# Softmax reciprocals spread through a row in HBM, and a sixth pair of heads in split fp32r products, in a fused attention and MLP layer

## The reference

```python
h = _layernorm(x) * (1 + ca) + sa
x = x + ga * attn(h)          # 16 query heads of 64, 4 key/value heads, rotary embedding
h = _layernorm(x) * (1 + cb) + sb
x = x + gb * ffn(h)           # binarised 128 -> 512 -> 128, exact gelu
# in attn: softmax(q k^T / 8) v, heads joined, @ Wo + bo
```

## Time and profile before

| | |
|---|---|
| median of three runs | 700.91 us (699.69 to 700.97) |
| profiled execution, its own time | 700.25 us |
| its span, first to last instruction | 698.5 us |
| PE matmul busy | 668.9 us, 96% |
| ACT busy | 551.4 us, 79% |
| DVE busy | 516.5 us, 74% |
| POOL busy | 430.1 us, 62% |
| DMA traffic on the SP queue | 24.40 MB |

### The profile page before, as it was taken

One profiled execution on the slowest core, in us unless ns is written; L12 is line 12 of the kernel. 1 busy time (PEld: TensorE's weight loads), 2 busy tenths in 40 slices (PEclk: granted clock), 3 DMA queues, 4 the chain that ended last, 5 costly groups with the idle time before them and its releaser, 6 DMA issues.

```text
span 698.5 us, 13530 instructions
## 1 busy us (share of the span) xinstructions
PE 668.9 (96%) x3733; PEld 519.5 (74%) x3733; DVE 516.5 (74%) x1196; ACT 551.4 (79%) x1149; POOL 430.1 (62%) x397
## 2 busy tenths in 40 slices
PE   4698999999999999999999999999999999998897
PEld 3566787877777787878787777778787878667786
DVE  6566777778788777777787778887777877778762
ACT  4478887888787888878887878787887888768676
POOL 1657685857686776768585768577676758543110
PEclk9699999999999999999999999999999999999999
DMA  8111111011111111111102111111111110200111
GB/s 241 31 32 33 33 26 39 18 38 28 32 31 32 32 20 29 32 32 32 31 16 43 20 32 31 32 32 28 26 27 33 32 34 18 48 17 3 39 39 46
DMA packets 31580, 24.75 MB, mean 35 GB/s; under 512 B 16688, under 2 KB 26944, under 8 KB 31552
## 3 DMA queue, kind: packets, MB, share of 16 engines
q1 hardware_dynamic: 31552, 24.40, 16.6%
HBM read 4.47 MB, written 2.10 MB: 9 GB/s over the span
## 4 chain that ended last, share of the span: by engine, by line
PE 90%; DVE 3%; ACT 3%; POOL 1%; issue 1%; DMA 0%; SPq 0%; POOLq 0%; DVEq 0%
PE o_ps L1021 15%; PE o_ps L1011 11%; PE unit_ps L957 9%; PE score_ps L992 8%; PE unit_ps L946 8%; PE score_ps L994 8%; PE unit_ps L973 8%; PE o_ps L1078 4%; PE unit_ps L931 3%; PE unit_ps L932 3%; PE unit_ps L933 3%; PE unit_ps L967 2%; PE unit_ps L961 2%; PE unit_ps L1055 1%; PE unit_ps L1056 1%
## 5 line engine op out<-in xcount | busy, mean ns | idle before, releaser
L521 POOL TENSOR_TENSOR probs_lo<-probs,probs_hi 128x512 fp32r<-128x512 f32 x160 | 202.1, 1283 | 67.7 <-ACT probs_hi L662 67.6
L772 DVE TENSOR_REDUCE w_all<-unit_ps 128x2 f32<-128x512 f32 x256 | 166.2, 685 | 52.4 <-PE unit_ps L957 50.9
L659 ACT ACTIVATE probs<-score_ps 128x512 f32<-128x512 f32 x256 | 150.6, 589 | 21.2 <-PE score_ps L994 18.6
L507 POOL TENSOR_TENSOR rot_sum<-rot_a,rot_b 128x512 f32<-128x512 f32 (+1 forms) x96 | 104.7, 1097 | 99.3 <-DVE rot_b L764 99.0
L511 POOL TENSOR_TENSOR qk_rot<-rot_sum,qk_rot 128x512 fp32r<-128x512 f32 (+1 forms) x96 | 105.0, 1101 | 36.3 <-ACT qk_rot L609 36.3
L957 PEld LDWEIGHTS unit_ps<-k_hi,q_hilo 128*128 128x128 f32 x512 | 88.7, 191 | 41.3 <-issue 17.9
L957 PE MATMUL unit_ps<-k_hi,q_hilo 128*128 128x256 f32 x512 | 118.3, 318 | 0.7 <-ACT q_hilo L591 0.4
L946 PEld LDWEIGHTS unit_ps<-ident_r,qk_rot 128*128 128x128 f32 x640 | 101.9, 194 | 17.7 <-issue 4.3
L946 PE MATMUL unit_ps<-ident_r,qk_rot 128*128 128x128 f32 x640 | 110.2, 264 | 4.6 <-POOL qk_rot L511 3.8
L992 PE MATMUL score_ps<-q_hilo,k_hi 128*128 128x512 f32 x256 | 112.9, 441 | 1.1 <-DMA q_him<-neg_max_t 1.1
L777 DVE TENSOR_TENSOR o_t<-o_un,unit_ps 64x256 f32<-64x256 f32 x248 | 103.5, 417 | 4.4
(11 more groups left out here) (120 smaller groups left out, 1123.4 us busy)
## 6 DMA issues: line engine op xcount, KB each, us to landing
q_him<-q_hilo SPq DMA_DIRECT2D x64, 256.0 KB
out_x<-w_all SPq DMA_DIRECT2D x16, 128.0 KB, 1.8
xa<-in_L_attn_x SPq DMA_DIRECT2D x3, 640.0 KB, 7.5
q_him<-neg_max_t SPq DMA_DIRECT2D x64, 4.0 KB
w_all<-in_L_attn_Wq SPq DMA_DIRECT2D x1, 512.0 KB, 5.3
w_sb<-in_L_ffn_w SPq DMA_DIRECT2D x2, 256.0 KB, 3.0
wo_sb<-in_L_attn_Wo SPq DMA_DIRECT2D x1, 512.0 KB, 8.2
sums<-o_un SPq DMA_DIRECT2D x32, 8.0 KB, 2.0
```

The lines of the kernel that those rows point to most:

```text
L507: pool.tensor_tensor(total, rot_a[k % 2][:, 0:heads, :], rot_b[k % 2][:, 0:heads, :], ALU.add).then_inc(rot_summed, 1)
L521: pool.tensor_tensor(probs_lo[s % 2][:, jc, :, :], probs[s % 2][:, jc, :, :], probs_hi[s % 2][:, jc, :, :].bitcast(F32), ALU.subtract).the ...
L659: ins = act.activation(probs[s % 2][:, jc, :, :].rearrange("p h i -> p (h i)"), score_ps[jc][:, :], ACT.Exp, scale=SCALE)
L772: dve.tensor_reduce(neg_max[u[1] // 4][:, first:first + C], ps[:, :].rearrange("p (c j) -> p c j", c=C), AX.X, ALU.max, negate=True).then_ ...
```

## The change

The products `bc`, the matrix `select` and the high and low parts of the reciprocals go. In their place SP copies the reciprocals of four pairs (8 KB) to a row in HBM, `recip_rows`, waits for it, and reads the row back twice by DMA with a broadcast, once into partitions 0 to 63 and once into 64 to 127 of `o_t`. `o_un` gets 128 partitions: ACT still writes both heads of a pair to partitions 0 to 64, and a further DMA of 256 KB (`second_heads`) copies the second heads to partitions 64 to 127. DVE then multiplies two pairs at a time over 128 partitions (words `mul0` to `mul3`). Pair 2 becomes a split pair. The order of the slots is written anew for this.

```diff
 SLOTS = [
-    "S0 s4 s5 m s6 m s7 xT0 xT0 m m S1 m qt4 qt4 m mT1 qt4 qt4",
-    "S0 m s8 S1 m qkv02 qt5 qt5 qt5 qt5 qkv12 m m m m",
-    "S0 s9 m recip1 s10 qt6 qt6 qt6 qt6 m S1 s11 m m m m qkv00 mT2",
-    "qkv10 S0 m s12 m m S1 bc4 bc5 qt7 qt7 qt7 qt7 m bc6 m m s13",
-    "S0 bc7 S1 m s14 m s15 kt0 m kt0 stats kt0 rstd kt0 kt1 norm m m kt1 kt1 kt1 m mT3 yT0",
-    "S0 qkv01 m m S1 m qt0 yT1 recip0 qt0 m qt0 m qt0 m",
-    "qt1 S0 qt1 qt1 qt1 s0 qt2 qt2 S1 qt2 s1 qt2 m s2 m s3 m zT0 zT0 m m m qkv11 mT0",
-    "S0 S1 bc0 m bc1 bc2 m m qt3 qt3 qt3 qt3 m m bc3 m",
+    "s4 S0 s5 s6 m s7 m xT0 xT0 mul0 m mul1 S1 m m m mT1",
+    "S0 m qkv02 qt4 qt4 qkv12 m qt4 qt4 qt5 m qt5 S1 qt5 m m qt5 m s8",
+    "S0 m recip1 s9 s10 m m S1 s11 qt6 m qt6 qkv00 qt6 m qt6 mT2 m",
+    "S0 s12 m m S1 qkv10 kt0 m m qt7 qt7 qt7 qt7 kt0 mul2 m kt0 s13 kt0 m mul3",
+    "S0 m s14 m s15 S1 kt1 m stats kt1 m rstd kt1 m kt1 m yT0 mT3",
+    "S0 qkv01 yT1 m m norm S1 qt0 m qt0 m qt0 qt0 m qt1 qt1 recip0 qt1 qt1 m qt2 qt2 zT0 zT0 qt2 qt2",
+    "S0 s0 m s1 s2 m m m s3 S1 m m qkv11 mT0",
+    "S0 qt3 S1 qt3 m qt3 m qt3 m m m m",
 ]
...
-SPLIT_PAIRS = (1, 3, 4, 5, 7)
+SPLIT_PAIRS = (1, 2, 3, 4, 5, 7)
...
-        o_un = sb("o_un", [DH + 1, PAIRS, 2, N])
+        o_un = sb("o_un", [P, 2, 2, 4, N])
...
+            def second_heads(st, half, batch):
+
+                sp.wait_ge(sums_in[half], st.count(16, 16, batch))
+                sp.dma_start(o_un[DH:P, half, 0, :, :].rearrange("p s i -> p (s i)"),
+                             o_un[0:DH, half, 1, :, :].rearrange("p s i -> p (s i)")).then_inc(second_in[half], 16)
+
+            def reciprocals_to_row(st, half, batch):
+
+                sp.wait_ge(recip_ready, st.count(2, half + 1, batch))
+                sp.dma_start(recip_rows[half].rearrange("h (b t) -> (h b) t", t=16),
+                             recip[:, :]).then_inc(rows_in[half], 16)
+
+            def reciprocals_to_all(st, half, batch):
+
+                sp.wait_ge(rows_in[half], st.count(16, 16, batch))
+                if half == 0 and not st.prep:
+                    sp.wait_ge(z_ready, B - 1)
+                for h in range(2):
+                    sp.dma_start(o_t[h * DH:h * DH + DH, 4 * half:4 * half + 4, :].rearrange("p s i -> p (s i)"),
+                                 recip_rows[half, h:h + 1].broadcast_to([DH, 4 * N])).then_inc(recip_in[half], 16)
...
                 if st.out:
-                    spread_reciprocals(st, 1, -1)
+                    second_heads(st, 1, -1)
+                    reciprocals_to_row(st, 1, -1)
+                    reciprocals_to_all(st, 1, -1)
                 if st.attn:
                     maxima(st, 2, 0)
                     high_parts(st, 3, 0)
                     maxima(st, 3, 0)
                     gather_sums(st, 0, 0)
-                    spread_reciprocals(st, 0, 0)
+                    second_heads(st, 0, 0)
+                    reciprocals_to_row(st, 0, 0)
                 if st.prep:
                     high_parts(st, 0, 1)
+                if st.attn:
+                    reciprocals_to_all(st, 0, 0)
+                if st.prep:
                     maxima(st, 0, 1)
                     high_parts(st, 1, 1)
...
+                            if st.number != 0 and pair < 4:
+                                act.wait_ge(o_t_ready, st.count(4, pair // 2 + 1, -1))
...
+            def normalise_heads(st, quarter, batch):
+
+                half, two = quarter // 2, slice(2 * quarter, 2 * quarter + 2)
+                own = slice(quarter % 2 * 2, quarter % 2 * 2 + 2)
+                if quarter % 2 == 0:
+                    dve.wait_ge(second_in[half], st.count(16, 16, batch))
+                    dve.wait_ge(recip_in[half], st.count(32, 32, batch))
+                dve.tensor_tensor(o_t[:, two, :], o_un[:, half, 0, own, :], o_t[:, two, :], ALU.mult).then_inc(o_t_ready, 1)
```

More of the change, by code:

```diff
@@ L85, in parsed @@
                 product += 1
[L86 removed]
+            elif kind in ("stats", "rstd", "norm", "recip", "mul"):
                 slot.append((kind, int(number or 0)))
@@ L210, in slot_parts @@
         parts = [("part", u, part, part == PARTS[u[0]] - 1) for _, u in units(st, s) for part in range(PARTS[u[0]])]
-        return [("recip", 1)] * (s == TAIL_RECIPROCALS_AT) + parts
+        return ([("recip", 1)] * (s == TAIL_RECIPROCALS_AT)
+                + [("mul", 2), ("mul", 3)] * (s == TAIL_PRODUCTS_AT) + parts)
     held = {"scores": st.attn, "pv": st.attn if s >= 1 else st.out, "un": st.attn if s >= 2 else st.out,
-            "stats": st.norm, "rstd": st.norm, "norm": st.norm}
+            "stats": st.norm, "rstd": st.norm, "norm": st.norm, "recip": (st.attn, st.out), "mul": (st.out,) * 4}
     return [w for w in ORDER[s]
-            if (not st.tail and has(st, w[1]) if w[0] == "part" else not st.tail and (st.attn, st.out)[w[1]] if w[0] == "recip"
+            if (not st.tail and has(st, w[1]) if w[0] == "part" else held[w[0]][w[1]] and not (st.tail and s > 1 - w[1] // 2) if w[0] in ("recip", "mul")
                 else held[w[0]])]
@@ L321, in adaln_layer @@
         q_hilo = [sb(f"q_hilo{i}", [P, HEADS, N], F32R) for i in range(2)]
-        q_him = [sb(f"q_him{i}", [DH + 1, 4, N], F32R) for i in range(2)]
+        q_him_all = sb("q_him_all", [P, 8, N], F32R)
+        q_him = [q_him_all[:, 4 * i:4 * i + 4, :] for i in range(2)]
+        recip_rows = nc.dram_tensor("recip_rows", (2, 2, 4 * N), F32, kind="Internal").ap()
         neg_max_t = [sb(f"neg_max_t{i}", [4 * C, P], F32R) for i in range(2)]
@@ L553, in _ @@
             act.activation(ident_r[:, :], ident[:, :], ACT.Copy).then_inc(ident_r_ready, 1)
-            for half in range(2):
-                act.activation(select[32 * half:32 * half + 32, :, :],
-                               ident[0:32, 0:PAIRS].unsqueeze(2).broadcast_to([32, PAIRS, DH]), ACT.Copy).then_inc(select_ready, 1)
             act.wait_ge(wkv_in, 16)
@@ L566, in unit @@
                 kind, ps, par = u[0], (tail_ps if st.tail else unit_ps)[bank(st, place)], st.par(ahead(u))
-                if kind in ("s", "zT", "bc") or (kind == "qkv" and u[2] != 2) or u == ("yT", 0):
+                if kind in ("s", "zT") or (kind == "qkv" and u[2] != 2) or u == ("yT", 0):
                     return
@@ L773, in unit @@
                                       ALU.max, negate=True).then_inc(max_ready, 1)
-                if kind == "bc":
-                    for h in range(2):
-                        ins = dve.tensor_tensor(o_t[h * DH:h * DH + DH, u[1], :], o_un[0:DH, u[1], h, :],
-                                                ps[h * DH:h * DH + DH, 0:N], ALU.mult)
-                    ins.then_inc(o_t_ready, 1)
                 if kind == "zT":
@@ L901, in wait_for_reader @@
                     pe.wait_ge(max_t_ready, st.count(4, u[1] + 1, of))
-                if kind == "bc":
-                    pe.wait_ge(o_t_ready, st.count(8, u[1] + 1, of))
                 if kind == "yT":
@@ L961, in unit @@
                     ins = pe.transpose(ps[:, 0:P], neg_max[u[1]], ident[:, :])
-                if kind == "bc":
-                    half = u[1] // 4
-                    if u[1] % 4 == 0:
-                        pe.wait_ge(recip_in[half], st.count(32, 32, ahead(u)))
-                    ins = pe.matmul(ps[:, 0:N], select[:, 2 * (u[1] % 4):2 * (u[1] % 4) + 2, :].rearrange("k h d -> k (h d)"),
-                                    recip_parts[half][:, :], start=True, stop=True)
                 if kind == "yT":
-                    pe.wait_ge(o_t_ready, st.count(8, 0))
+                    pe.wait_ge(o_t_ready, st.count(4, 0))
                     own = slice(u[1] * P, (u[1] + 1) * P)
```

52 lines of the change are left out of this document (19 added, 33 removed).

## The result

The changed kernel takes 757.32 us (median of 4 runs, 752.57 to 768.29), the kernel before beside it 700.42 (699.69 to 700.97): a ratio of 1.079, 95% interval 1.072 to 1.086. The ratio goes by the three lower runs; the fourth, 768.29, counts as disturbed. The forecast was 695, faster. The profiled execution took 752.57 around a span of 750.8. From the page of the changed kernel: busy time per engine, then three groups (busy, mean ns of one, idle before them).

The account below looks back on a forecast made before the run. PE's matmuls bound each step of 37.71 us; 1.5 leaves PE, a floor of 36.2, which takes 700.9 to 677 us. New waits of 1.2 in each of 15 steps add 18: 695 us, range 677 to 712.

Parts of the forecast that it names:

- What bounds the kernel: Steady step: it lasts as long as PE's matmuls, 37.69 of 37.71 us; the other engines have 6 to 12 to spare.
- What leaves PE: PE per step: bc −0.96, pair 2 −0.32, reordered transpositions −0.25, together −1.5; floor 36.2 us, 677 without new waits.
- What the others take on: Busy time per step on ACT 32.1, POOL 28.7, DVE about 24 us; none becomes the bound as a sum.
- Wait 1: kt0 in slot 3 waits for a rotation that POOL finishes late, behind four low parts: 0.75 us a step.
- Wait 2: S0 of slot 4 waits for maxima(2), queued on SP behind the two broadcasts: 0.5 us a step.
- rival 2: maxima(2) land behind two slow broadcasts and S0 of slot 4 waits 2.4 a step: 713 us; chance 0.20.
- rival 1: PE stays full, POOL and broadcast early enough, waits under 0.5 a step: 677 to 684, say 680; chance 0.22.
- The multiplies: DVE's mul2 and mul3 beside busy POOL: nothing to 1.25 us longer each, taken as 0.05 of PE wait a step.
- Rival 3: POOL and DVE hold each other up at multiplies and low parts, 0.5 a step more: 703 us; chance 0.13.

Follow-up runs that it names:

- e11: Changed kernel with recip1 in slot 1, second heads and row issued before high parts 2, S1 ahead of qkv02, no POOL pauses: 671.76 us, ratio 0.959.
- e12: e6 with recip1 in slot 1 and the row ahead of high parts 2, no POOL pauses: 675.96 us, ratio 0.965.
- e5: Kernel before the change with pair 2 split and nothing else: 708.07 us, ratio 1.011.
- e8: Changed kernel with recip1 in slot 1, second heads and row before high parts 2, S1 ahead of qkv02, POOL pausing for mul2 and mul3: 692.26 us.
- e2: Changed kernel with POOL pausing for mul2 and mul3, and SP sending maxima(2) ahead of the two broadcasts: 700.33 us.
- e1: Changed kernel with POOL waiting for mul2 and mul3 before it goes on: 698.69 us, ratio 0.998 of the kernel before.
- e3: Changed kernel with the multiply replaced by a reduce that reads o_un alone, leaving the division out: 690.7 us, ratio 0.986.
- e4: Kernel without the layer: five kinds of DVE instruction started inside POOL trains; the product of two SBUF operands took 0.63 to 1.11 us.
- e6: Changed kernel with pair 2 in plain fp32 products again, slots as they are: 690.14 us, ratio 0.985.
- e13: Changed kernel with a DVE memset of 128x64 between the wait for the broadcast and mul2: 759.89 us, 8 of 14 mul2 long.
- e14: Changed kernel with SP issuing only second_heads ahead of high parts 2: 682.42, 685.33, 695.55 and 709.54 us in four runs.
- e15: Changed kernel run once more, unaltered: 763.7 us, 8 of 14 mul2 long.

## Why the prediction was wrong

**What bounds the kernel.** Right. The steps are made of PE's work, and e11 and e12 show steps that are nothing but that.

**What leaves PE.** Right in kind, and a little too careful: the floor was 36.2 a step, and e11, whose PE is full, has 35.90 and takes 672 us, where 677 was forecast without new waits. e12 has pair 2 plain, so its floor by the same count is 36.5; it measured 36.24. A small part of this is the count of transpositions that directly follow another one: by the prediction's own rule the slot texts give 22 before and 15 after, −0.35 a step, not 23, 18 and −0.25. Pair 2 was counted at 0.32, and e11 and e12 differ by 0.32; in the order before (e5) it brought nothing. The short steps of the changed kernel have 36.41 of PE work and 0.9 of waits, the forecast had 36.2 and 1.2, so that the 695 comes out again is in part two errors that cancel.

**What the others take on.** Right in size: POOL forecast at 28.7, in the short step 29.3; ACT 32.1, measured 31.8; DVE about 24, measured 26.0 with the waits inside the multiplies.

**Wait 1.** The mechanism was right, the size 0.4 to 0.5 instead of 0.75: e8 removed it by the cause named, POOL's order. **Wait 2.** Also right, 0.3 to 0.5 for 0.5; the view names no releaser for it, and that it is the maxima is shown by e2, which moved them and removed it. The uncertain price in it, the two broadcasts, was 4.8 us for an estimated 4.3. They landed only 0.3 later than forecast, because SP issued them 0.2 earlier, so rival 2 (a late broadcast, 713) had next to nothing in it. A full PE (rival 1) was not seen in the changed kernel, and its two waits are indeed what e11 had to remove for it.

**The multiplies.** The step that failed. It said: "The new multiplies are of that kind, and POOL is always busy then. Bounds: nothing, or 1.25 for each of the two", and took 0.05. The rows had shown the mechanism (1.21 us for 16 columns, ending with POOL's instruction), and e1 and e3 show that it is the one that matters. The upper bound was wrong: it supposed that the loser waits for one POOL instruction. What the runs showed is a loser that stays out to the end of that instruction and over the five behind it, until POOL is idle, in half of the steps; 6.9 us for 1.25, and with PE's wait and the lower clock behind it 8.2 us on the step where I had 0.05. Rival 3, which ends on the right side, was the right mechanism at a price that was 0.5 a step for a measured mean of 4.1 (58 / 14), so its 703 missed the 757 too, and the range, which ended at 712, with it.

The bound should have been the train, not the instruction. The rows gave a wait that ended with an instruction, but the trace of the kernel before also had the other kind, `var_eps` at 546.76, which passed over a boundary and ended with the train, and its view by source (168/510/2268) showed it. POOL's order stood in my own working for wait 1 ("From here POOL is never free"). The way to POOL's next pause, which measured some 7 us, could have been worked out as the end of the range.

The Trainium skill (SBUF — State Buffer, "Who interferes with whom") has which forms compete with GpSimd: a DVE instruction with two SBUF inputs, and a copy, a cast or a `tensor_scalar` where it can enter a mode that takes both ports, but not a reduce; and whoever starts first holds the pair to its end. The runs agree in which ones are held: the reduce of e3 and e4 and the product from PSUM stay at one fixed time, the copy goes up to 0.83 instead of 0.36, and `var_eps`, a `tensor_scalar`, is held. They don't agree in the length: read as it stands, that rule lets a multiply wait for one POOL instruction, 1.28, as in the three kernels without the layer; in the layer it waited for up to 8.5. POOL's loss was near what the prediction took from the rule: 0.45 to each multiply that got in, for 0.6.

**What stays open.** Why the first boundary is lost in the layer, by `mul2` in about half of the steps and by `var_eps` in all of e3, and never outside, or by `mul3`, or by the 42 `mul2` of e6, e11 and e12. Excluded by runs as what it takes: the release by a DMA (e13), one particular boundary (e14), the program by itself (e15), and, by `var_eps`, a second operand, a large operand or a DVE that stood idle before. The point within POOL's instruction at which `mul2` starts showed no pattern. A product written into another tile inside the layer was not tried. That an instruction which lost one boundary loses until POOL idles is a reading of all 26 long `mul2` and of `var_eps` in e3, but why isn't settled.

## What to carry to other kernels

Price an instruction by where its operands lie and by its operation as well as by its size: in this layer a DVE product with both operands in SBUF beside a busy GpSimd, and even an addition of a constant to 128x2, had as its upper bound the way to GpSimd's next pause, and whatever is queued behind it on DVE has that bound too. A held instruction is busy in the profile and no wait, so compare the maximum of its group with its minimum; a mean of 1631 ns for a size that takes 674 was the plainest sign of it on the page. To cure it, bring what it waits for earlier, so that it lands beside another train (e11, −86 us), before adding pauses to the other engine: they cure it too, but cost 20 us more (e8 against e11). That `mul2` of e11 also stands behind other work of DVE is no protection by itself, since `var_eps` stood behind such work in e3 and lost. Without the shut-out the rest of the change was worth 29 us, the 24 that had been counted and a few more.
